# A mixture-of-experts stage whose odd last block of 128 rows joins the last full tile

## Chip, cores and metric

The kernel runs on 1 core of one Trainium2 chip. The metric is device microseconds of one execution, median of several runs.

## What is computed

An adaLN block: layer norm, modulation by rows of `mod`, a gated linear recurrence with projections (the first part, not touched here), a second layer norm, and a mixture of 8 experts with 2 chosen per token. The touched part is the experts:

```
gate_scores = softmax(x @ Wg + bg)
topk_scores, topk_idx = top_k(gate_scores, 2)       # normalized to sum 1
for e in range(8):
    h = gelu(x @ W1[e] + b1[e])                     # 256 -> 1024
    y = h @ W2[e] + b2[e]                           # 1024 -> 256
    output = output + y * combine_w[..., e:e + 1]
x = x + gb * output
```

x has 4 x 1024 tokens of 256 values, float32. The gate's bias is large in these inputs, so the experts get very different numbers of tokens.

## The kernel before

The first part sorts tokens by expert: each token's row goes twice, by an indirect DMA, into a DRAM table `disp_x`, at its place in its expert's region. The second part walks over the experts n = 0 to 7 and over the tiles of each. A tile is TE = 256 rows, two blocks of 128. How many tiles an expert has is known only on the chip: `counts` on DVE packs the numbers, and every engine reads them into registers (`counts_of`, `count_of`) and runs the same loop, `tile(True, 2)`, a hardware loop over `tile(False, 2)`, and, if the number of blocks is odd, `tile(False, 1)` (lines 258 to 267). Each engine has its own copy of `tile`, and they meet at semaphores; `due(name, by)` raises a register and waits for the semaphore to reach it.

In one tile:

- **SP** (388 to 395) loads the rows of the tile into `xin`, one tile ahead, and with an expert's first tile the weights of the expert after next.
- **PE** (932 to 944): layer 1 for f = 0 to 7, six matmuls each (two halves k of the contraction, times three products of high and low parts, because each operand is split into two fp32r numbers), into `mm[f % 4]`, always TE = 256 columns, for an odd block too. Layer 2 follows four f behind, three matmuls per block of 128 rows and f, into `yb`. Behind layer 2 of f = 4 stands `turn()`: four transposes of the next tile's rows into `tp`. Then layer 2 of f = 5, 6, 7.
- **ACT** (743 to 755): two gelus per f, `h32` (double buffered) and its rounded form `hh`; in an expert's first tile a high part of the next expert's weights with f = 4 to 7; at the end `fh`, the high part of the turned rows.
- **DVE** (1256 to 1305): per f the low part `hl`, a small operation on the weights of the tokens, and in an expert's first tile splits of the next expert's weights (`SH` 229, `SL` 237). At the end `fl`, the low part of the turned rows (1239); then a wait for `gbr`, the copy of the rows' last columns (`xm`, 1244), `ytmp` (1295, layer 2 plus bias) and per block `ysb` (1304).
- **POOL** (561 to 578): in an expert's first tile three splits of the next expert's weights (237); then per block an indirect DMA that adds `ysb` to the rows of `out_x` (543), and between the two the gathers of `gbr` for the next tile (538).

What orders the work around the change: POOL's queue holds splits, adds and gathers in program order, two adds never run at once (`y_sent0`, `y_sent1`), and PE's second layer needs `hl` from DVE and an empty `yb` (`y_taken`).

## Time and profile before

| | |
|---|---|
| median of 3 runs | 799.66 us (799.52 to 799.69) |
| profiled execution | 806.43 us |
| its span | 804.6 us |
| TensorE clock granted, mean | 0.942 |
| PE matmul busy | 716.1 us, 89% |
| DVE busy | 559.6 us, 70% |
| ACT busy | 419.0 us, 52% |
| POOL busy | 403.9 us, 50% |

The expert stage begins at about 336.7 us of the span and lasts to its end. Matmuls are pipelined, and the busy time of one is longer than the distance to the next, so a busy TensorE does not tell how fast it goes; distances between starts do. The granted clock is 1.00 at 2.4 GHz and 0.50 at 1.2 GHz.

### The profile page before, as it was taken

What the parts mean: (1) busy time and instruction counts of PE and PEld (TensorE: products, weight loads), DVE (VectorE), ACT (ScalarE), POOL (GpSimd) and SP (SyncE); (2) the same over time, 40 slices, a digit from 0 to 9 for tenths busy, and PEclk for the clock granted to TensorE, in tenths of its full rate; (3) what the DMA queues carried; (4) which work ended last, traced back from release to release, by engine and by line L of the source; (5) the groups of instructions that cost most, each with busy time, mean ns of one, the idle gap of its engine ahead of it and who ended that gap; (6) DMA issues with size and microseconds to landing.
All of it is one profiled execution on the core that took longest, in us unless ns stands there. A gap on an engine that the chain in (4) does not pass through costs nothing.

```text
span 804.6 us, 17323 instructions
## 1 busy us (share of the span) xinstructions
PE 716.1 (89%) x4850; PEld 659.4 (82%) x4850; DVE 559.6 (70%) x1786; ACT 419.0 (52%) x1080; POOL 403.9 (50%) x312
## 2 busy tenths in 40 slices
PE   4999999889799992479999999999898998999992
PEld 1777888778688872369999899998898998999992
DVE  6789888998888659565555755576875576585551
ACT  6365565445455261155665565664554574565660
POOL 1364637666562744734544534554653553553543
PEclk9899999999999995599999999999898999999997
DMA  8531103020101206414455334564532553533432
GB/s 289 185 106 53 54 33 114 28 81 28 53 28 55 81 21 218 166 48 68 71 118 127 60 58 75 117 170 117 154 59 54 118 127 67 106 61 68 65 69 41
DMA packets 50165, 72.56 MB, mean 90 GB/s; under 512 B 5792, under 2 KB 41964, under 8 KB 49968
## 3 DMA queue, kind: packets, MB, share of 16 engines
q0 software_dynamic: 16480, 27.28, 18.5%
q1 hardware_dynamic: 33616, 44.46, 17.5%
q8 instruction: 30, 0.49, 0.3%
q14 instruction: 39, 0.32, 0.1%
HBM read 48.85 MB, written 22.87 MB: 89 GB/s over the span
## 4 chain that ended last, share of the span: by engine, by line
PE 63%; DVE 20%; issue 8%; DMA 3%; ACT 2%; POOL 2%; DVEq 0%; SPq 0%; POOLq 0%; ACTq 0%
PE mm L917 21%; PE yb L927 19%; PE mm L773 14%; PE yb L798 4%; DVE hl L1273 2%; PE tp L900 2%; DMA gbr<-mod_rows,xm 2%; DVE SL L237 1%; DVE nt L954 1%; DVE nt L950 1%; DVE bst L959 1%; PE tp L823 1%; DVE rsn L955 1%; DVE ob L1022 1%; DVE SH L229 1%
## 5 line engine op out<-in xcount | busy, mean ns | idle before, releaser
L750 ACT ACTIVATE h<-mm,b1T 128x256 f32<-128x256 f32 (+1 forms) x288 | 134.2, 466 | 190.8 <-PE mm L917 130.5
L1273 DVE TENSOR_TENSOR hl<-h,hh 128x256 fp32r<-128x256 f32 (+1 forms) x288 | 126.0, 442 | 141.7 <-ACT hh L751 111.5
L543 POOL DMA_INDIRECT out_x<-ysb,tokb x68 | 113.3, 1666 | 204.0 <-DVE ysb L1304 166.4
L917 PE MATMUL mm<-fh,SH 128*128 128x256 f32 x576 | 167.9, 291 | 16.4 <-DVE fl L1239 13.8
L927 PE MATMUL yb<-SH,hh 128*128 128x256 f32 x544 | 158.1, 291 | 10.4 <-DVE hl L1273 10.0
L917 PE MATMUL mm<-fl,SH 128*128 128x256 f32 x576 | 166.0, 288 | 0.0
L917 PE MATMUL mm<-fh,SL 128*128 128x256 f32 x576 | 165.7, 288 | 0.0
L927 PE MATMUL yb<-SH,hl 128*128 128x256 f32 x544 | 154.2, 284 | 0.6 <-issue 0.6
L927 PE MATMUL yb<-SL,hh 128*128 128x256 f32 x544 | 153.5, 282 | 0.0
L751 ACT ACTIVATE hh<-mm,b1T 128x256 fp32r<-128x256 f32 (+1 forms) x288 | 133.5, 464 | 0.0
L917 PEld LDWEIGHTS mm<-fh,SH 128*128 128x128 f32 x576 | 114.2, 198 | 19.1 <-issue 18.4
L773 PE MATMUL mm<-xh,WH 128*128 128x512 f32 x256 | 109.0, 426 | 6.4 <-DVE ob L1022 4.2
L917 PEld LDWEIGHTS mm<-fl,SH 128*128 128x128 f32 x576 | 113.8, 198 | 0.0
L927 PEld LDWEIGHTS yb<-SH,hh 128*128 128x128 f32 x544 | 103.2, 190 | 12.8 <-DVE hl L1273 12.0
L917 PEld LDWEIGHTS mm<-fh,SL 128*128 128x128 f32 x576 | 113.6, 197 | 0.0
L927 PEld LDWEIGHTS yb<-SH,hl 128*128 128x128 f32 x544 | 103.5, 190 | 0.7 <-issue 0.7
L927 PEld LDWEIGHTS yb<-SL,hh 128*128 128x128 f32 x544 | 103.6, 190 | 0.0
L773 PE MATMUL mm<-xh,WL 128*128 128x512 f32 x256 | 103.2, 403 | 0.0
L773 PE MATMUL mm<-xl,WH 128*128 128x512 f32 x256 | 102.7, 401 | 0.0
L538 POOL DMA_INDIRECT gbr<-mod_rows,xm x74 | 76.9, 1039 | 22.6 <-issue 22.6
L498 POOL DMA_INDIRECT disp_x<-h2all,pos x64 | 62.7, 980 | 30.6 <-issue 27.5
L773 PEld LDWEIGHTS mm<-xh,WH 128*128 128x128 f32 x256 | 49.8, 195 | 17.7 <-issue 5.8
(213 smaller groups left out, 1214.9 us busy)
## 6 DMA issues: line engine op xcount, KB each, us to landing
xin<-disp_x SPq DMA_DIRECT2D x74, 132.0 KB
wraw<-in_L_ffn_W SPq DMA_DIRECT2D x8, 1024.0 KB
h2all<-in_L_ffn_W SPq DMA_DIRECT2D x8, 1024.0 KB
xb<-in_L_attn_x SPq DMA_DIRECT2D x8, 512.0 KB, 6.7
out_x<-x2b SPq DMA_DIRECT2D x8, 512.0 KB
mb<-mod_rows SPq DMA_DIRECT2D x3, 768.0 KB, 6.4
wraw<-in_L_attn_W_ugg SPq DMA_DIRECT2D x1, 1536.0 KB, 10.0
gbr<-mod_rows,xm POOLq DMA_INDIRECT x74
```

Source lines behind the costliest of these rows:

```text
L229: e.tensor_copy(SH[n % 2][:, r], wraw[n % 2][:, r]).then_inc(done, 1)
L498: e.indirect_dma_start(out=Xd, out_offset=bass.IndirectOffsetOnAxis(ap=p[:, j:j + 1], axis=0), in_=h2all[:, j, :], in_offset=None).then_in ...
L538: e.indirect_dma_start(out=gbr[:, j, :], out_offset=None, in_=modd.rearrange("b (n d) -> (b n) d", d=D), in_offset=bass.IndirectOffsetOnAx ...
L543: e.indirect_dma_start(out=out_rows, out_offset=bass.IndirectOffsetOnAxis(ap=tokb[:, j:j + 1], axis=0), in_=ysb[:, j, :], in_offset=None, ...
L750: e.activation(h32[:, f % 2, c_], mm[f % 4][:, c_], ACT.Gelu_apprx_tanh, bias=bias)
L751: e.activation(hh[:, f, c_], mm[f % 4][:, c_], ACT.Gelu_apprx_tanh, bias=bias)\
L773: i = e.matmul(mm[q][:, :], a[:, k, c0:c0 + 128], b[:, g % 2, k, :], start=(k == 0 and t == 0), stop=(k == 1 and t == 2))
L798: i = e.matmul(yb[j // 2][:, (j % 2) * D:(j % 2 + 1) * D], og[:, n % 2, j * 128:(j + 1) * 128], wog[:, (g // 2) % 2, hc, :], start=(hc == ...
L900: i = e.transpose(tp[k][:, j * 128:(j + 1) * 128], xin[:, j, k * 128:(k + 1) * 128], ident[:, :])
L917: i = e.matmul(mm[f % 4][:, 0:TE], a[:, k, f * 128:(f + 1) * 128], b[:, k, :], start=(k == 0 and t == 0), stop=(k == 1 and t == 2))
L927: i = e.matmul(yb[0][:, j * D:(j + 1) * D], a[:, f, j * 128:(j + 1) * 128], b[:, f, :], start=(f == 0 and j == 0 and t == 0), stop=(f == N ...
L1273: e.tensor_tensor(hl[:, f, w_], h32[:, f % 2, w_], hh[:, f, w_].bitcast(F32), ALU.subtract)\
```

## The change

A tile with three blocks takes the place of a full tile and an odd one. `count_of` takes one full tile away from the loop when the count of blocks is odd, and behind the loop stands `tile(False, 3)`. Buffers get a third block (`xin`, `xm`, `gbr`, `ysb`, `ytmp` and so on) or 384 columns (`fh`, `fl`, `h32`, `hh`, `hl`, T3 = 384). The third block's rows are loaded with the two others, but turned and split into high and low when the joined tile begins, since the turn at the end of a tile is the same code for all. Layer 1 of f = 0 is cut in 256 and 128 columns, so that it can begin before the third block is there; f = 1 to 7 run over 384 columns. The third block's second layer goes to `yb[1]`. POOL gathers the third `gbr` at the tile's start and makes three adds, then waits for the third to land.

```
@@ -253,6 +256,8 @@
             e.reg_alu(k, half, 1, ALU.logical_shift_right)
             e.reg_alu(k, k, 15, ALU.bitwise_and)
             e.reg_alu(half, half, 1, ALU.bitwise_and)
+            e.reg_alu(k, k, half, ALU.subtract)
+            e.reg_alu(k, k, 1, ALU.max)
             return e.snap(k, min_val=1, max_val=CAP // TE - 1), half
 
         def more_tiles(e, rs, n, tile):
@@ -260,7 +265,7 @@
             with e.Fori(0, k):
                 tile(False, 2)
             with e.If_ne(half, 0):
-                tile(False, 1)
+                tile(False, 3)
 
         def tiles(e, rs, n, tile):
...
@@ -387,6 +392,8 @@
 
                 def tile(first, parts):
                     load(rows_of)
+                    if parts == 3:
+                        e.dma_start(xin[:, 2, :], rows_of(2)).then_inc(S["third_loaded"], 16)
                     if first and n == 0:
                         e.wait_ge(S["counts_ready"], 2)
                         e.reg_load(r_last, nmint[0:1, n:n + 1])
...
+            def gather_gb(j, name):
+                e.indirect_dma_start(out=gbr[:, j, :], out_offset=None, in_=modd.rearrange("b (n d) -> (b n) d", d=D),
+                                     in_offset=bass.IndirectOffsetOnAxis(ap=xm[:, j, 5:6].bitcast(I32), axis=0))\
+                    .then_inc(S[name], 16)
 
             def gather():
...
@@ -562,20 +572,24 @@
                     if first and n + 1 < E:
                         for q in range(5, 8):
                             split_low(e, n + 1, q)
+                    if parts == 3:
+                        due("third_copied", 1)
+                        gather_gb(2, "third_gb")
                     due("y_ready", 1)
                     if not (first and n == 0):
                         due("y_sent0", 0)
                         due("y_sent1", 0)
                     add(0)
-                    if parts == 2:
+                    due("y_ready", 1)
+                    gather()
+                    due("y_sent0", 16)
+                    add(1)
+                    e.reg_add(rl["y_sent1"], rl["y_sent1"], 16)
+                    if parts == 3:
                         due("y_ready", 1)
-                    gather()
-                    if parts == 2:
-                        due("y_sent0", 16)
-                        add(1)
-                        e.reg_add(rl["y_sent1"], rl["y_sent1"], 16)
-                    else:
-                        e.reg_add(rl["y_sent0"], rl["y_sent0"], 16)
+                        due("y_sent1", 0)
+                        add(2)
+                        due("y_sent2", 16)
 
                 tiles(e, ks, n, tile)
             due("gb_loaded", 32)
...
+            def third_part():
+                for k in range(2):
+                    due("third_turned", 1)
+                    e.activation(fh[:, k, TE:T3], tp[k][:, TE:T3], ACT.Copy).then_inc(S["third_high"], 1)
 
             e.reg_mov(rl["rows_turned"], 2)
             e.sem_inc(S["gelu_done"], 4)
@@ -742,6 +761,8 @@
             for n in range(E):
                 def tile(first, parts):
                     c_ = slice(0, 128 * parts)
+                    if parts == 3:
+                        third_part()
                     for f in range(NF):
                         due("layer1_done", 1)
...
@@ -910,12 +931,22 @@
                 w2h, w2l = (t[s][:, 2048:4096].rearrange("p (c n) -> p c n", c=NF) for t in (SH, SL))
                 split_done(e, n)
 
+                def turn_third():
+                    due("third_loaded", 16)
+                    for k in range(2):
+                        e.transpose(tp[k][:, TE:T3], xin[:, 2, k * 128:(k + 1) * 128], ident[:, :])\
+                            .then_inc(S["third_turned"], 1)
+
                 def layer1(f, parts):
                     due("gelu_done", 1)
-                    for k in range(2):
-                        for t, (a, b) in enumerate(((w1h, fh), (w1h, fl), (w1l, fh))):
-                            i = e.matmul(mm[f % 4][:, 0:TE], a[:, k, f * 128:(f + 1) * 128], b[:, k, :],
-                                         start=(k == 0 and t == 0), stop=(k == 1 and t == 2))
+                    cuts = (0, 128 * parts) if parts == 2 or f else (0, TE, T3)
+                    for c0, c1 in zip(cuts, cuts[1:]):
+                        if c0:
+                            due("third_low", 2)
+                        for k in range(2):
+                            for t, (a, b) in enumerate(((w1h, fh), (w1h, fl), (w1l, fh))):
+                                i = e.matmul(mm[f % 4][:, c0:c1], a[:, k, f * 128:(f + 1) * 128], b[:, k, c0:c1],
+                                             start=(k == 0 and t == 0), stop=(k == 1 and t == 2), skip_group_check=True)
                     i.then_inc(S["layer1_done"], 1)
 
                 def layer2(f, parts):
@@ -924,13 +955,15 @@
                     due("hidden_low", 1)
                     for j in range(parts):
                         for t, (a, b) in enumerate(((hh, w2h), (hh, w2l), (hl, w2h))):
-                            i = e.matmul(yb[0][:, j * D:(j + 1) * D], a[:, f, j * 128:(j + 1) * 128], b[:, f, :],
-                                         start=(f == 0 and j == 0 and t == 0), stop=(f == NF - 1 and t == 2),
+                            i = e.matmul(yb[j // 2][:, j % 2 * D:(j % 2 + 1) * D], a[:, f, j * 128:(j + 1) * 128], b[:, f, :],
+                                         start=(f == 0 and j != 1 and t == 0), stop=(f == NF - 1 and t == 2),
                                          skip_group_check=True)
                     i.then_inc(S["layer2_done"], 1)
 
                 def tile(first, parts):
                     due("rows_low", 2)
+                    if parts == 3:
+                        turn_third()
                     for f in range(NF):
                         layer1(f, parts)
                         if f >= 4:
...
+            def third_part():
+                for k in range(2):
+                    due("third_high", 1)
+                    e.tensor_tensor(fl[:, k, TE:T3], tp[k][:, TE:T3], fh[:, k, TE:T3].bitcast(F32), ALU.subtract)\
+                        .then_inc(S["third_low"], 1)
 
+
+            def third_columns():
+                due("third_loaded", 16)
+                e.tensor_copy(xm[:, 2, :], xin[:, 2, D:DW]).then_inc(S["third_copied"], 1)
 
...
+                        5: lambda: e.tensor_scalar(nom[:, 0:2], nom[:, 0:2], float(TE), None, ALU.add),
+                        6: lambda: e.tensor_copy(tokn[:, 0:parts], xm[:, 0:parts, 4].bitcast(I32)),
                     }
                     if first:
-                        mark(e.tensor_scalar(nom[:, :], nom0, float(n * CAP), None, ALU.add))
+                        mark(e.tensor_scalar(nom[:, 0:2], nom0, float(n * CAP), None, ALU.add))
                         due("dve_c", 1)
+                    if parts == 3:
+                        third_columns()
+                        mark(e.tensor_scalar(nom[:, 2:3], nom[:, 1:2], 128.0, None, ALU.add))
+                        third_part()
+                        due("dve_c", 1)
...
@@ -1292,13 +1341,17 @@
                     due("gb_loaded", 32)
                     columns()
                     due("layer2_done", NF)
-                    e.tensor_tensor(ytmp[:, 0:parts, :], yb[0][:, 0:parts * D].rearrange("p (j d) -> p j d", j=parts),
-                                    bc(b2b[:, n, :], parts), ALU.add).then_inc(S["y_taken"], 1)
+                    i = e.tensor_tensor(ytmp[:, 0:2, :], yb[0][:, :].rearrange("p (j d) -> p j d", j=2),
+                                        bc(b2b[:, n, :], 2), ALU.add)
+                    if parts == 3:
+                        i = e.tensor_tensor(ytmp[:, 2, :], yb[1][:, 0:D], b2b[:, n, :], ALU.add)
+                    i.then_inc(S["y_taken"], 1)
                     due("y_taken", 1)
                     for j in range(parts):
-                        sent = "y_sent1" if j else "y_sent0"
-                        if not (first and n == 0):
-                            due(sent, 16)
+                        if j < 2 and not (first and n == 0):
+                            due(f"y_sent{j}", 16)
+                        if j == 2:
+                            due("third_gb", 16)
                         mark(e.tensor_copy(tokb[:, j:j + 1], tokn[:, j:j + 1]))
                         due("dve_c", 1)
                         e.scalar_tensor_tensor(ysb[:, j, :], ytmp[:, j, :], wB[:, j:j + 1], gbr[:, j, :],

```

The new order at the places concerned follows, first POOL, around the end of an expert whose count is odd and the start of the next one. Before, the odd tile's add and gathers and then the splits:

```order
L262 COMPARE_AND_BRANCH
...
L543 DMA out_x<-ysb,tokb 4096x256 [waits s_y_ready,s_y_sent0,s_y_sent1]
...
L538 DMA gbr<-mod_rows,xm 128x256 [waits s_meta_copied]
L538 DMA gbr<-mod_rows,xm 128x256
...
L262 UNCONDITIONAL_BRANCH
L237 TENSOR_TENSOR SL<-wraw,SH 128x512 [waits s_split_high2] x3
```

After, the joined tile and then the same splits (line numbers are those of the changed file; L553 is the add, L543 the gather):

```order
L543 DMA gbr<-mod_rows,xm 128x256 [waits s_third_copied]
...
L553 DMA out_x<-ysb,tokb 4096x256 [waits s_y_ready,s_y_sent0,s_y_sent1]
...
L281 REGISTER_ALU [waits s_y_ready]
L543 DMA gbr<-mod_rows,xm 128x256 [waits s_meta_copied]
L543 DMA gbr<-mod_rows,xm 128x256
...
L553 DMA out_x<-ysb,tokb 4096x256 [waits s_y_sent0]
...
L281 REGISTER_ALU [waits s_y_ready]
L553 DMA out_x<-ysb,tokb 4096x256 [waits s_y_sent1]
...
L267 UNCONDITIONAL_BRANCH [waits s_y_sent2]
L240 TENSOR_TENSOR SL<-wraw,SH 128x512 [waits s_split_high2] x3
```

Between the last gather and the splits there are now two more adds and a wait for a landing.

Second, PE at the start of that tile. Before, the odd tile's first layer follows the branch directly:

```order
L262 COMPARE_AND_BRANCH
L276 REGISTER_ALU
L276 REGISTER_ALU [waits s_rows_low]
L917 MATMUL mm<-fh,SH 128x256 [waits s_gelu_done]
L917 MATMUL mm<-fl,SH 128x256
```

After:

```order
L281 REGISTER_ALU [waits s_rows_low]
L937 MATMUL tp<-ident,xin 128x128 [waits s_third_loaded]
L937 MATMUL tp<-ident,xin 128x128
L281 REGISTER_ALU
L948 MATMUL mm<-fh,SH 128x256 [waits s_gelu_done]
...
L948 MATMUL mm<-fh,SH 128x128 [waits s_third_low]
...
L948 MATMUL mm<-fh,SH 128x384 [waits s_gelu_done]
L948 MATMUL mm<-fl,SH 128x384
```

The 128-column matmuls wait for DVE's subtraction, and all of the first layer from f = 1 on stands behind them. On DVE that subtraction stands behind the last tile's output:

```order
L1357 SCALAR_TENSOR_TENSOR ysb<-ytmp,wB,gbr 128x256 [waits s_dve_c]
...
L267 COMPARE_AND_BRANCH
...
L1287 COPY xm<-xin 128x8 [waits s_third_loaded]
L1315 TENSOR_SCALAR nom<-nom 128x1
...
L1278 TENSOR_TENSOR fl<-tp,fh 128x128 [waits s_third_high]
...
L1278 TENSOR_TENSOR fl<-tp,fh 128x128 [waits s_third_high]
```

Before, DVE went from `ysb` straight to `hl` of the next tile.

## Rows read from the trace of the kernel before

**Rows 1.** Groups by line and form: name, count, busy us, mean ns, idle before

```profile
L1295 DVE TENSOR_TENSOR ytmp<-yb,x2b 128x512 f32<-128x512 f32 x32 | 22.1, 691 | 19.2 <-PE yb L927 19.2
L1295 DVE TENSOR_TENSOR ytmp<-yb,x2b 128x256 f32<-128x256 f32 x4 | 1.7, 424 | 0.0
```

**Rows 2.** Windows: length, us busy (count) of PE, PEld, DVE, ACT, POOL; PEclk

```profile
425.23:435.17 9.94, 9.94 (x87) 9.94 (x86) 5.32 (x22) 4.92 (x16) 4.05 (x4) 1.00 0.72 173
435.17:446.69 11.52, 11.21 (x93) 10.81 (x92) 9.54 (x25) 9.31 (x24) 7.34 (x6) 1.00 0.47 83
446.69:462.53 15.84, 13.96 (x102) 13.26 (x101) 10.54 (x28) 6.95 (x19) 7.23 (x6) 0.89 0.28 54
462.53:474.26 11.73, 11.73 (x103) 11.73 (x102) 6.55 (x23) 6.47 (x17) 5.01 (x4) 1.00 0.29 55
```

**Rows 3.** Windows, last row and sum: odd turn to next, then next to second

```profile
700.04:712.36 12.32, 11.18 (x93) 10.78 (x92) 9.40 (x27) 8.95 (x24) 7.30 (x6) 1.00 0.47 80
sum 46.90, PE 44.78 PEld 43.17 DVE 36.97 ACT 36.34 POOL 27.74; mean PE 11.20 PEld 10.79 DVE 9.24 ACT 9.08 POOL 6.93
...
712.36:727.66 15.30, 13.81 (x102) 13.41 (x101) 9.95 (x26) 7.48 (x20) 7.33 (x6) 0.89 0.30 53
sum 62.38, PE 54.98 PEld 53.29 DVE 42.62 ACT 28.57 POOL 31.24; mean PE 13.74 PEld 13.32 DVE 10.66 ACT 7.14 POOL 7.81
```

**Rows 4.** Timeline, PE: start us, length us; nine and 29 matmuls between the pairs

```profile
99.72 0.39 PE L773 MATMUL mm<-xl,WH 128*128 128x512 f32 x1
...
101.78 0.39 PE L773 MATMUL mm<-xl,WH 128*128 128x512 f32 x1
...
427.79 0.28 PE L917 MATMUL mm<-fh,SH 128*128 128x256 f32 x1
...
431.18 0.27 PE L917 MATMUL mm<-fh,SL 128*128 128x256 f32 x1
```

**Rows 5.** Timeline, PE: two stops, idle before in brackets

```profile
449.73 0.38 PE L927 MATMUL yb<-SH,hh 128*128 128x256 f32 x1 [1.73 <-DVE hl L1273]
...
605.88 0.58 PE L917 MATMUL mm<-fh,SH 128*128 128x256 f32 x1 [3.81 <-DVE fl L1239]
```

**Rows 6.** Timeline, DVE, around expert 0's odd tile and expert 1's first

```profile
427.99 0.69 DVE L1295 TENSOR_TENSOR ytmp<-yb,x2b 128x512 f32<-128x512 f32 x1 [1.09 <-PE yb L927]
...
429.00 0.48 DVE L1304 SCALAR_TENSOR_TENSOR ysb<-ytmp,wB,gbr 128x256 f32<-128x256 f32 x1
...
430.04 0.49 DVE L1273 TENSOR_TENSOR hl<-h,hh 128x128 fp32r<-128x128 f32 x2
...
437.85 0.18 DVE L1244 COPY xm<-xin 128x16 f32<-128x16 f32 x1 [0.56 <-DMA gbr<-mod_rows,xm]
...
438.70 0.48 DVE L1304 SCALAR_TENSOR_TENSOR ysb<-ytmp,wB,gbr 128x256 f32<-128x256 f32 x1
...
444.38 4.37 DVE L1264 TENSOR_SCALAR nom<-nom 128x2 f32<-128x2 f32 x1
```

**Rows 7.** Timeline, POOL, the same stretch

```profile
430.64 1.56 POOL L543 DMA_INDIRECT out_x<-ysb,tokb  x1 [4.92 <-DVE ysb L1304]
...
433.82 0.99 POOL L538 DMA_INDIRECT gbr<-mod_rows,xm  x1 [0.30 <-issue]
...
435.50 1.61 POOL L543 DMA_INDIRECT out_x<-ysb,tokb  x1 [0.69 <-issue]
...
440.33 1.71 POOL L543 DMA_INDIRECT out_x<-ysb,tokb  x1 [3.22 <-DMA out_x<-ysb,tokb]
...
444.94 3.77 POOL L237 TENSOR_TENSOR SL<-wraw,SH 128x512 fp32r<-128x512 f32 x3
```

**Rows 8.** POOL's adds into out_x, from issue to landing

```profile
DMA to landing us min/median/max: 3.7/3.9/4.7
```

**Rows 9.** Windows behind two stops, columns as in the second group

```profile
451.55:454.60 3.05, 2.94 (x14) 2.65 (x14) 2.34 (x8) 0.68 (x2) 0.00 (x0) 0.50 0.33 83
...
605.88:611.38 5.50, 5.50 (x26) 5.50 (x27) 2.89 (x9) 2.52 (x6) 2.58 (x2) 0.50 0.36 69
```

More of the change, by code:

```diff
@@ L20 @@
 TE = 256
+T3 = 384
 MW = 8
@@ L537, in gather @@
                 for j in range(2):
-                    e.indirect_dma_start(out=gbr[:, j, :], out_offset=None, in_=modd.rearrange("b (n d) -> (b n) d", d=D),
-                                         in_offset=bass.IndirectOffsetOnAxis(ap=xm[:, j, 5:6].bitcast(I32), axis=0))\
-                        .then_inc(S["gb_loaded"], 16)
+                    gather_gb(j, "gb_loaded")
             def add(j):
```

62 lines of the change are left out of this document (31 added, 31 removed).

## Prediction

> **What bounds the kernel.** I read the page first: TensorE is busy for most of the span, but that figure hides where it waits, so the expert stage has to be cut by tiles. The DVE line that adds the second layer's bias runs once a tile and has one form per kind of tile: 32 full tiles and 4 of one block [rows 1]. Its start times give the experts: experts 0, 1, 4 and 5 end in an odd block, the other four do not. So the change acts at four places.
>
> Next the windows between turns (the transposes of the next tile's rows, once a tile on PE) [rows 2]. T is a turn's time. From turn to turn a full tile has 96 matmuls and takes 11.73 us (11.72 in most others), 9.94 us when the 81 matmuls between the turns before and in an odd tile are meant. The pitch from one matmul start to the next is (431.18 - 427.79) / 29 = 0.117 us at 256 columns and (101.78 - 99.72) / 9 = 0.229 us at 512 [rows 4]. So 96 x 0.1175 = 11.28 us, and 0.44 us is left for a turn: PE is the bound in a steady tile, with no slack of its own.
>
> What breaks this are two stretches after an odd block [rows 2, 3]. From the odd tile's turn to the next, 87 matmuls should take 10.66 us; the four stretches sum to 46.90, 4.26 us too much. The odd tile's second layer leaves 9 matmuls (1.1 us) behind the turn, less than the copy and subtraction of the turned rows take. From the first tile's turn of the next expert to the second's, the four sum to 62.38, 15.5 us over four steady tiles: PE stops for hl [rows 5], because DVE's instruction stood for 4.37 us [rows 6] while POOL ran its three splits in 3.77 us [rows 7]. After such a stop the granted clock is 0.50, that is 1.2 GHz in place of 2.4, for a while [rows 9].
>
> **The change, part by part.**
>
> (a) Matmuls. An odd tile goes: 48 + 24 matmuls of 256 columns and a turn, 72 x 0.1175 + 0.44 = 8.90 us. Its 24 second-layer matmuls come back in the joined tile (2.82 us). Of the first layer 42 matmuls grow to 384 columns; midway between 0.117 and 0.229 is 0.173, so 42 x 0.056 = 2.35 us. Six of 128 columns are new; no row shows that form, so the bounds are half of 0.117 and 0.117, and I take 0.09 (0.54 us). Two transposes, 0.2 us. Together 5.9 us, so 3.0 us are saved per odd block, 12.0 in all. This is real PE time and nothing hides it.
>
> (b) The short tail. The joined tile has 27 matmuls behind its turn instead of 9 (3.2 us), more than the fh and fl chain needs. The 4.26 us go: -4.3.
>
> (c) The third block's rows, a new wait. They are turned only when the joined tile begins, and DVE subtracts them only behind the last tile's output. In a full tile ytmp starts at T + 2.76, ysb at T + 3.77, and DVE's next instruction at T + 4.81 [rows 5, 6]. There the small copy and two subtractions of 128 columns come in (0.1 each for the small ones, about 0.25 each for the others), so fl is there at T + 5.6. PE has begun the tile at T + 2.56, and two transposes and six matmuls last it to T + 3.5. So it waits some 2.0 us. ACT and the DMA of the rows are no part of this: that load is issued a tile ahead. Behind the waiting PE instruction stand L1(1) to L1(4), which were what covered DVE's lateness before. Behind the stop of about 2 us at 449.73 came 14 matmuls at the half clock (3.05 / 14 = 0.218 us each) [rows 9], behind others of nearly that length none: 14 x 0.096 = 1.35 us, counted half, 0.65. Four times 2.65: +10.6.
>
> (d) POOL. An odd tile's POOL work ended with its gathers; nobody waited for its add. The joined tile ends in three adds, each waiting for the landing of the one before, and a wait for the last landing, and behind that stand the three splits of the next expert, the next tile's add and its gathers. From the joined tile's turn T' on: 27 matmuls, ytmp at T' + 3.9; the extra block puts the first ysb at T' + 5.3; add 0 comes 1.6 us after its ysb (438.70 to 440.33 in that tile, and 429.00 to 430.64 here [rows 6, 7]): T' + 6.9. Add 1 follows 4.8 later (430.64 to 435.50 [rows 7], with two gathers inside): T' + 11.7. Landing takes 3.9 us [rows 8] and about 0.6 more until POOL's next: add 2 at T' + 16.2, last landing seen at T' + 20.7. Splits 3.9: T' + 24.6. The next tile's add 0 at 24.8, second gather 3.2 after it (430.64 to 433.82) at 28.0; it lands 4.0 later (DVE stood for the one of 433.82 until 437.85 [rows 6, 7]): T' + 32.0. DVE, in the second tile of the next expert, wants it at about T' + 26 and has nothing to do instead. Then ytmp, ysb 0 (33.2), the landing of add 1 (24.8 + 4.8 + 4.3 = 33.9), ysb 1, and hl for the third tile is ready at T' + 35.0. PE undisturbed would want it at T' + 3.7 + 2 x 11.72 + 5 x 6 x 0.1175 = T' + 30.7. That is 4.3 us of standing still, and like the 3.81 us stop of 605.88 it should be followed by 26 matmuls at 0.50, 5.50 / 26 = 0.21 us each in place of 0.1175 [rows 5, 9]: 26 x 0.096 = 2.5. So 6.8 us a time, 27.2 for four. Against that the old stalls of the first tiles go, 15.5, since the splits no longer fall there. In expert 5 the late tile is itself a joined one and PE meets the wait five matmul groups sooner, about 1 us more. Together +12.7.
>
> Costed at nothing: wider gelus (ACT 0.36 to about 0.47 us each, two per 2.1 us of PE), wider hl, and SP's third load per joined tile, which SP issues with a tile's time in hand. If that cover went, 6 x 0.2 us would show.
>
> Sum: -12.0 - 4.3 + 10.6 + 12.7 = **+7.0 us**. Against the profiled execution (806.43 us, a span of 804.6 and 1.8 around it) that is 813.4; that execution is 6.8 above the median of the runs, and I carry the difference over: 799.66 + 7.0 = 806.7.
>
> **The rivals.**
>
> R1, the price of POOL's chain is about that of the old stalls. Each link in (d) has a spread of about half a microsecond and there are four; if all are short, the stop is 2 to 2.5 us and the clock seldom falls. Then (d) is near zero and the rest gives -5.7: 794. For it: landings reach down to 3.7 [rows 8]. Against: nothing in the chain overlaps.
>
> R2, the other side in full: the chain is absorbed. The place is DVE's wait for the gathers in the second tile of the next expert, the price 6.8 us each, and it decides at T' + 30.7: if the chain is over 4.3 us shorter, old stalls of 15.5 us disappear and only a lateness of 1 us in the first tile is left. Then -12.0 - 4.3 + 10.6 - 15.5 + 4 = -17: 782. For it: DVE has half its time free. Against: the rows of landings. The Trainium skill, "DMA: Bandwidth & Descriptors", section "Anatomy of one DMA", puts the fixed part of a transfer, setup and completion, at some 2.0 us. By that, four landings of 2 us would take 7.6 us off the chain and R2 would hold. The row of this trace has 3.7 at the least and 3.9 in the middle, so this rule of the Trainium skill does not fit these adds, and the measurement decides.
>
> R3, worse than forecast: dependent adds come at over 5 us, or expert 2, which has only two tiles, carries the lateness into the first tile of expert 3, where DVE also splits weights. 2 to 3 us more per place: 816 and up.
>
> R4, the change is not taken (no odd block reaches the new branch): 799.7. The four forms of 256 columns speak against it [rows 1].
>
> **How the numbers follow.** Forecast 0.58, with a range of its own of 800.5 to 816; R1 0.18; R2 0.12; R3 0.10; R4 0.02. A measurement of this kernel can tell about 0.2%, 1.6 us, from no change. Faster takes R1 and R2: 0.30. Same takes R4 and the low edge of the forecast: 0.06. Slower: 0.64. The range reaches down to R1 and up to the edge of R3: 793 to 816; R2 and most of R3 stay outside.
>
> **What would show it.** (a) 36 turns become 32; matmuls of 384 columns with a pitch near 0.173. (b) no stop between joined tile and next expert but some tenths. (c) four stops of about 2 us in front of the 128-column matmuls, ended by DVE fl. (d) POOL's splits some 20 us behind the joined tile's turn, DVE's copy xm idle for 4 to 6 us on gbr in the second tile, PE idle about 4 us for hl or yb in the third. The forecast is wrong if the third tile after a joined one runs at 11.7 us, or if the stop in (c) is under 1 us.

## The result, and the profile after

| | before | after |
|---|---|---|
| median of 4 runs each | 799.67 us (799.52 to 801.37) | 815.06 us (813.57 to 817.61) |
| ratio | | 1.0193 (95% interval 1.0174 to 1.0211) |
| profiled execution | 806.43 us | 816.36 us |
| its span | 804.6 us | 814.6 us |
| TensorE clock granted, mean | 0.942 | 0.932 |
| TensorE matmul busy | 716.1 us, 89% | 711.4 us, 87% |

The change makes the kernel slower by 15.4 us in the medians and by 10.0 us between the two profiled executions. Forecast were +7.0 and a range of 793 to 816. So the sign held, the range held by 0.9 us, and the size was less than half of what came. For the profiled execution the forecast was 813.4 us, and it took 816.36. A second comparison, below, gave 1.0158. Two of all the runs below were in the chip's slower state (802.10 us in `e6_dve_cut4`, 1185.47 us in `e10_before_dve_again`), and the times and ratios leave them out.

In the changed program layer 1 is line 948, layer 2 line 958, `fl` 1272 and the third block's `fl` 1278, `hl` 1322, the copy `xm` 1283, `ysb` 1357, the splits 240, the adds 553 and the gathers 543.

The page of the changed kernel: its busy shares, and the chain of work that ended last.

```profile
span 814.6 us, 16564 instructions
...
PE 711.4 (87%) x4674; PEld 655.7 (80%) x4674; DVE 547.1 (67%) x1734; ACT 410.0 (50%) x1016; POOL 398.2 (49%) x308
...
PE 56%; DVE 15%; DMA 10%; issue 9%; POOL 6%; ACT 2%; POOLq 1%; SPq 0%; DVEq 0%; ACTq 0%
PE yb L958 17%; PE mm L948 16%; PE mm L794 14%; DMA out_x<-ysb,tokb 7%; PE yb L819 4%; POOL gbr L543 1%; POOL SL L240 1%; PE tp L921 1%; DVE rsn L988 1%; POOL disp_x L505 1%; DVE hl L1322 1%; DVE ob L1055 1%; DVE bst L992 1%; PE tp L844 1%;
```

TensorE is busy for 4.7 us less and the end comes 10 us later. The landing of an add into `out_x` is now 7% of the chain, some 57 us: the adds have become part of what sets the end. In the chain of before all DMA together had 3%.

The windows between turns: first the four joined tiles, from the turn ahead of each to its own T', then the turn to turn stretches behind the first of them (these answer to [rows 2, 3]). Columns: stretch, its length, busy time of PE, its weight loads, DVE, ACT and POOL, granted clock, DMA share, GB/s.

```profile
411.90:430.86 18.96, 17.18 (x126) 16.98 (x124) 8.40 (x27) 9.54 (x20) 7.41 (x6) 1.00 0.50 112
509.38:529.87 20.49, 18.71 (x125) 18.51 (x124) 8.41 (x27) 9.54 (x20) 8.15 (x6) 0.92 0.47 104
631.56:652.06 20.50, 18.72 (x126) 18.52 (x124) 8.40 (x27) 9.54 (x20) 6.74 (x6) 0.92 0.44 104
677.17:706.55 29.38, 20.16 (x126) 19.95 (x125) 8.82 (x27) 9.54 (x20) 14.54 (x12) 0.77 0.30 50
...
430.86:444.16 13.30, 13.15 (x111) 12.94 (x110) 9.95 (x33) 7.96 (x20) 5.31 (x4) 1.00 0.26 49
444.16:455.97 11.81, 11.81 (x103) 11.81 (x102) 9.87 (x23) 7.15 (x19) 6.05 (x5) 1.00 0.29 49
```

The third stretches, in which POOL's chain arrives:

```profile
455.97:473.96 17.99, 14.55 (x103) 14.35 (x102) 7.09 (x25) 7.78 (x20) 10.21 (x8) 0.81 0.46 73
555.04:573.88 18.84, 13.61 (x102) 13.12 (x101) 9.86 (x32) 8.03 (x20) 9.46 (x8) 0.91 0.66 177
731.65:750.54 18.89, 14.49 (x102) 14.29 (x101) 6.75 (x23) 7.48 (x20) 9.90 (x8) 0.82 0.44 71
```

Expert 5 has three tiles, so its third stretch is itself a joined tile, the one of 29.38 us. The first stretch (13.30) has nothing of the old idle in it, and the second runs at the steady pace, where before it cost 3.6 to 4.1 us more [rows 2]. The time comes back one tile later: 6.3 to 7.2 us above a steady tile of before.

TensorE's queue in the joined tile of expert 0, and in the third stretch behind it:

```profile
417.32 0.33 PE L948 MATMUL mm<-fh,SH 128*128 128x128 f32 x1 [1.78 <-DVE fl L1278]
417.48 0.28 PE L948 MATMUL mm<-fl,SH 128*128 128x128 f32 x1
...
417.94 0.27 PE L948 MATMUL mm<-fh,SL 128*128 128x128 f32 x1
...
418.27 0.34 PE L948 MATMUL mm<-fl,SH 128*128 128x384 f32 x1
...
419.86 0.34 PE L948 MATMUL mm<-fl,SH 128*128 128x384 f32 x1
...
465.69 0.58 PE L958 MATMUL yb<-SH,hh 128*128 128x256 f32 x1 [3.44 <-DVE hl L1322]
466.07 0.41 PE L958 MATMUL yb<-SL,hh 128*128 128x256 f32 x1
...
471.19 0.32 PE L958 MATMUL yb<-SL,hh 128*128 128x256 f32 x1
```

The stop in front of the 128-column matmuls is there. The pitch, the distance from one matmul's start to the next, is (419.86 - 418.27) / 9 = 0.177 us for 384 columns and (417.94 - 417.48) / 4 = 0.115 us for 128. Behind the 3.44 us stop the matmuls go at (471.19 - 466.07) / 24 = 0.213 us, the half clock, as in [rows 9].

What POOL does from T' = 430.86 on, in the order in which it comes:

```profile
437.67 1.58 POOL L553 DMA_INDIRECT out_x<-ysb,tokb  x1 [11.17 <-DVE ysb L1357]
...
442.35 1.62 POOL L553 DMA_INDIRECT out_x<-ysb,tokb  x1 [0.38 <-issue]
447.40 1.56 POOL L553 DMA_INDIRECT out_x<-ysb,tokb  x1 [3.43 <-DMA out_x<-ysb,tokb]
451.32 4.29 POOL L240 TENSOR_TENSOR SL<-wraw,SH 128x512 fp32r<-128x512 f32 x3 [2.36 <-DMA out_x<-ysb,tokb]
455.76 1.55 POOL L553 DMA_INDIRECT out_x<-ysb,tokb  x1 [0.16 <-issue]
...
458.93 0.99 POOL L543 DMA_INDIRECT gbr<-mod_rows,xm  x1 [0.30 <-issue]
```

and what DVE waits for meanwhile:

```profile
462.20 0.17 DVE L1283 COPY xm<-xin 128x16 f32<-128x16 f32 x1 [4.24 <-DMA gbr<-mod_rows,xm]
```

| link, us behind T' | forecast | here |
|---|---|---|
| add 0 | 6.9 | 6.8 |
| add 1 | 11.7 | 11.5 |
| add 2 | 16.2 | 16.5 |
| splits | 20.7 | 20.5 |
| next tile's first add | 24.8 | 24.9 |
| its second gather | 28.0 | 28.1 |
| copy `xm` | 32.0 | 31.3 |
| TensorE goes on | 35.0 | 34.8 |

Every link is within 0.7 us of the forecast here. The chain that starts in expert 4's joined tile and ends in expert 5's was slower. Its last add goes out together with SP's load of 1024 KB of weights, and POOL's splits then wait for that add to land:

```profile
669.69 1.57 POOL L553 DMA_INDIRECT out_x<-ysb,tokb  x1 [3.11 <-DMA out_x<-ysb,tokb]
669.71 0.43 SPq L300 DMA_DIRECT2D h2all<-in_L_ffn_W  x1
676.12 3.98 POOL L240 TENSOR_TENSOR SL<-wraw,SH 128x512 fp32r<-128x512 f32 x3 [4.85 <-DMA out_x<-ysb,tokb]
```

```profile
690.06 0.48 PE L948 MATMUL mm<-fh,SH 128*128 128x128 f32 x1 [9.22 <-DVE fl L1278]
```

There T' is 652.06. Adds 1 and 2 came at T' + 12.7 and 17.6 (11.7 and 16.2 forecast) and the splits at T' + 24.1 in place of 20.7: the add of 669.69 took 6.2 us to land, the longest of the 36 adds whose landing was traced, where the median is 3.8. The windows of the third add at the first place and at this one, columns as above, differ in what the DMA engines moved:

```profile
447.40:451.32 3.92, 3.92 (x35) 3.92 (x34) 2.56 (x9) 2.76 (x8) 1.56 (x1) 1.00 0.54 105
669.69:676.12 6.43, 6.43 (x57) 6.43 (x56) 3.81 (x14) 4.87 (x14) 1.57 (x2) 1.00 0.81 229
```

It was the same place in two more traces: in `c_after` the add of 673.03 took 5.4 us beside a load of 672.51, in `e1_wait_later` the add of 670.38 took 6.6 us beside a load of 670.83. So this is most likely the weight load in the way, and not the scatter of one execution; no run moved the load, so that is not shown.

### The profile page after: what moved, and what is told of

It is laid out like the page before. It is cut to its first block, busy times and chain, and to the rows that moved or that the text cites. A ratio compares the mean times of both kernels' runs of the same rounds, so it can differ in the third digit from the quotient of the medians.

```text
span 814.6 us, 16564 instructions
## 1 busy us (share of the span) xinstructions
PE 711.4 (87%) x4674; PEld 655.7 (80%) x4674; DVE 547.1 (67%) x1734; ACT 410.0 (50%) x1016; POOL 398.2 (49%) x308
## 3 DMA queue, kind: packets, MB, share of 16 engines
q1 hardware_dynamic: 33040, 43.92, 16.8%
## 4 chain that ended last, share of the span: by engine, by line
PE 56%; DVE 15%; DMA 10%; issue 9%; POOL 6%; ACT 2%; POOLq 1%; SPq 0%; DVEq 0%; ACTq 0%
PE yb L958 17%; PE mm L948 16%; PE mm L794 14%; DMA out_x<-ysb,tokb 7%; PE yb L819 4%; POOL gbr L543 1%; POOL SL L240 1%; PE tp L921 1%; DVE rsn L988 1%; POOL disp_x L505 1%; DVE hl L1322 1%; DVE ob L1055 1%; DVE bst L992 1%; PE tp L844 1%; POOL out_x L553 1%
## 5 line engine op out<-in xcount | busy, mean ns | idle before, releaser
L771 ACT ACTIVATE h<-mm,b1T 128x256 f32<-128x256 f32 (+1 forms) x256 | 125.4, 490 | 187.6 <-PE mm L948 138.8
L553 POOL DMA_INDIRECT out_x<-ysb,tokb x68 | 110.8, 1629 | 217.3 <-DVE ysb L1357 175.2
L1322 DVE TENSOR_TENSOR hl<-h,hh 128x256 fp32r<-128x256 f32 (+1 forms) x256 | 120.6, 476 | 115.9 <-ACT hh L772 113.7
L958 PE MATMUL yb<-SH,hh 128*128 128x256 f32 x544 | 159.3, 293 | 16.5 <-DVE hl L1322 16.5
L948 PE MATMUL mm<-fh,SH 128*128 128x256 f32 (+2 forms) x520 | 156.6, 301 | 19.5 <-DVE fl L1278 14.6
L948 PE MATMUL mm<-fh,SL 128*128 128x256 f32 (+2 forms) x520 | 154.7, 297 | 3.6 <-issue 3.6
L948 PE MATMUL mm<-fl,SH 128*128 128x256 f32 (+2 forms) x520 | 155.7, 299 | 0.0
L772 ACT ACTIVATE hh<-mm,b1T 128x256 fp32r<-128x256 f32 (+1 forms) x256 | 124.8, 488 | 0.0
L948 PEld LDWEIGHTS mm<-fh,SH 128*128 128x128 f32 x520 | 103.7, 200 | 24.7 <-DVE fl L1278 15.4
L948 PEld LDWEIGHTS mm<-fl,SH 128*128 128x128 f32 x520 | 103.5, 199 | 0.0
L948 PEld LDWEIGHTS mm<-fh,SL 128*128 128x128 f32 x520 | 103.5, 199 | 0.0
L543 POOL DMA_INDIRECT gbr<-mod_rows,xm x70 | 71.8, 1026 | 21.3 <-issue 21.3
## 6 DMA issues: line engine op xcount, KB each, us to landing
wraw<-in_L_attn_W_ugg SPq DMA_DIRECT2D x1, 1536.0 KB, 11.7
```

The lines of the kernel that those rows point to most:

```text
L543: e.indirect_dma_start(out=gbr[:, j, :], out_offset=None, in_=modd.rearrange("b (n d) -> (b n) d", d=D), in_offset=bass.IndirectOffsetOnAx ...
L553: e.indirect_dma_start(out=out_rows, out_offset=bass.IndirectOffsetOnAxis(ap=tokb[:, j:j + 1], axis=0), in_=ysb[:, j, :], in_offset=None, ...
L771: e.activation(h32[:, f % 2, c_], mm[f % 4][:, c_], ACT.Gelu_apprx_tanh, bias=bias)
L772: e.activation(hh[:, f, c_], mm[f % 4][:, c_], ACT.Gelu_apprx_tanh, bias=bias)\
L948: i = e.matmul(mm[f % 4][:, c0:c1], a[:, k, f * 128:(f + 1) * 128], b[:, k, c0:c1], start=(k == 0 and t == 0), stop=(k == 1 and t == 2), s ...
L958: i = e.matmul(yb[j // 2][:, j % 2 * D:(j % 2 + 1) * D], a[:, f, j * 128:(j + 1) * 128], b[:, f, :], start=(f == 0 and j != 1 and t == 0), ...
```

## The experiments

Each time stands beside runs of the kernel before on the same chip. That kernel took 798.7 to 807.0 us from one comparison to the next, so ratios are compared and not times. A ratio here is the recorded estimate with its 95% interval, which is not the plain quotient of the two medians. `c_before`, `e1_wait_later`, `e3_buffers` and `e4_before_dve` ran beside a kernel before of 805.79 us; `c_after`, `e2_cut4`, `e5_after_dve` and `e8_buffers_pad`, on the same chip, beside 807.00; `e6_dve_cut4`, `e10_before_dve_again` and a single run of `e11_hh_only`, on another chip, beside 804.64; and a single run of `e12_fh_only`, on a third one, beside 798.67.

**The two kernels again.** No edit.

> The kernel before once more, as a second profile of it. Both theories: ratio 1.000 within 0.002, a steady tile of 11.72 us from turn to turn, and again 15 to 16 us of excess over the four first tiles behind odd blocks. If the first profile of it was an unusual one (it was 6.8 us above the median), the stretch ahead of the experts or behind the last turn is 3 us shorter here, or a first tile ran without a clock drop.

> The changed kernel once more, beside the three others of this job and the kernel before on one chip. Both theories: ratio 1.012 to 1.020, turns of the tiles behind a joined one 13.3, 11.8 and 18 to 19 us apart, an extra 10 us in expert 5's joined tile.

The kernel before against itself: 805.47 us, ratio 1.000 (0.9978 to 1.0022). The changed kernel: 819.5 against 807.0 us, ratio 1.0158 (1.0106 to 1.0211). So these comparisons can tell about 0.2% to 0.6%, depending on how many runs they have, and the loss is there again: 12.5 us in the medians. In the trace of `c_after` the first three joined tiles took 18.95, 18.97 and 18.97 us: the same stop in front of the 128-column matmuls each time (1.76 to 1.78 us idle), and no half clock behind it. In the trace of the changed kernel two of three had one (20.49, 20.50).

**Does the chain of waits set the late stop?** The changed kernel; POOL waits for the third block's landing behind the next expert's splits, not ahead of them.

```
@@ POOL, tile @@
+                    if first and n:
+                        due("y_sent2", 0)
...
                         add(2)
-                        due("y_sent2", 16)
+                        e.reg_add(rl["y_sent2"], rl["y_sent2"], 16)
...
+            due("y_sent2", 0)
```

> The changed kernel, with POOL's wait for the landing of the third add moved behind the three splits of the next expert. Theory (POOL's chain sets the stop in the third tile): splits start some 4 us sooner, at about T' + 16.7, the gather of the second tile lands 4 us sooner, and the stop of 3.4 us and more in the third tile goes. But the splits then fall on the ysb and the first hl of the second tile, DVE stands for 4 us there, and PE stops some 3 us in the second tile instead, with a half clock behind it in most: about 803 us, ratio 1.005. Rival (the third tile's lateness comes from DVE's own longer list behind a joined tile): the stop stays where it is, 815 us.

814.08 us, ratio 1.0101 (1.0066 to 1.0135). Windows behind the first joined tile, columns as above, and the three instructions that matter:

```profile
418.26:437.22 18.96, 17.18 (x126) 16.98 (x124) 8.51 (x27) 9.52 (x20) 8.23 (x6) 1.00 0.52 113
437.22:450.53 13.31, 13.16 (x112) 12.95 (x110) 9.96 (x33) 7.78 (x20) 5.37 (x4) 1.00 0.26 50
450.53:467.92 17.39, 13.66 (x102) 13.31 (x101) 11.94 (x25) 8.26 (x21) 10.68 (x8) 0.90 0.35 56
```

```profile
454.30 4.80 DVE L1360 SCALAR_TENSOR_TENSOR ysb<-ytmp,wB,gbr 128x256 f32<-128x256 f32 x1
```

```profile
454.51 4.29 POOL L240 TENSOR_TENSOR SL<-wraw,SH 128x512 fp32r<-128x512 f32 x3
```

```profile
460.75 0.58 PE L961 MATMUL yb<-SH,hh 128*128 128x256 f32 x1 [3.73 <-DVE hl L1325]
```

The stop left the third stretch and came a tile earlier, into the second. The splits now run while DVE makes `ysb`, and DVE's instruction takes 4.80 us in place of 0.48. So the place of the splits decides where TensorE stands, and an earlier place only trades the wait for a landing against the shut-out of [rows 6, 7]. In expert 5 the joined tile took 20.50 us in place of 29.38. I had expected a ratio of about 1.005; each second stretch cost 5.1 to 5.6 us over a steady one (17.39, 17.24, 16.86 and 17.06 us), more than I had counted for it.

**Without POOL's splits.** In both kernels the low parts q = 5, 6, 7 of the next expert's weights move from POOL to DVE, behind `columns()` and ahead of `ytmp` in the first tile.

```
@@ POOL, tile @@
-                    if first and n + 1 < E:
-                        for q in range(5, 8):
-                            split_low(e, n + 1, q)
@@ DVE, tile @@
+                    if first and n + 1 < E:
+                        for q in range(5, 8):
+                            split_low(e, n + 1, q)
```

> The changed kernel with the three low parts moved from POOL to DVE, as in the run that gave 0.971 for the kernel before. Theory (POOL's chain of adds, landings and splits makes the stop in the third tile): without the splits the chain is 4.1 us shorter, hl is ready at T' + 31 against a need at T' + 31, so the third tile has a stop of less than 1 us and no half clock, and no first tile has the old stops. From 0.971 come off 12 us of matmuls and 4 of short tail, and on it come 7 of stops in the joined tiles, 4 of clock and 2.5 of buffers: about 0.968. Rival (the joining itself costs time somewhere else, in the joined tile or on the queues): 0.98 or more, still 9 us or so above what the kernel before has with the same move.

> The kernel before, with the three low parts of the next expert's weights (q = 5, 6, 7) computed by DVE, behind its copy xm in an expert's first tile, in place of POOL. Theory (the old stops come from DVE being shut out while POOL splits): the stops of 1.7 to 3.8 us and the half clocks behind them go in all first tiles, some 25 us in all, less a small lateness of ytmp, since 1.9 us of DVE work meet 1.1 us of idle time there: 774 to 780 us, ratio 0.97 to 0.975. Rival (the first tile is simply too much for DVE): the 1.9 us come on top and the stops stay, near 800 or above.

> The kernel before with DVE's low parts, run again beside the last one on the same chip. Both theories: ratio 0.967 to 0.976. If the run with both remedies is below it by more than the intervals, joining pays; if the two are within 0.3%, it pays nothing here.

Changed kernel so edited: 794.34 us, ratio to the kernel before 0.9848 (0.9795 to 0.99). Kernel before so edited: 784.22 us, 0.9713 (0.9666 to 0.9761), and again on another chip 787.60 us, 0.9751 (0.9691 to 0.981). This is the best version of the study, faster than both kernels; I had expected 0.97 to 0.975. Windows of both, from the full tile ahead of expert 0's last block. The kernel before so edited (odd tile, then two stretches of expert 1):

```profile
437.21:448.62 11.41, 11.21 (x94) 10.81 (x93) 8.93 (x30) 9.02 (x24) 5.49 (x4) 1.00 0.53 81
448.62:460.46 11.84, 11.84 (x102) 11.78 (x101) 8.78 (x26) 6.52 (x17) 4.48 (x4) 1.00 0.33 60
460.46:472.21 11.75, 11.75 (x103) 11.75 (x102) 6.45 (x22) 6.96 (x18) 6.13 (x5) 1.00 0.43 71
```

The changed kernel so edited (joined tile, then three stretches; last the joined tile of expert 5):

```profile
417.79:438.33 20.54, 18.73 (x125) 18.53 (x124) 8.39 (x27) 9.53 (x20) 7.03 (x6) 0.92 0.48 103
438.33:451.65 13.32, 13.17 (x111) 12.96 (x110) 9.96 (x33) 7.79 (x20) 5.39 (x4) 1.00 0.29 50
451.65:464.55 12.90, 12.30 (x103) 11.94 (x102) 9.29 (x28) 8.17 (x21) 5.55 (x4) 1.00 0.38 58
464.55:476.36 11.81, 11.81 (x103) 11.81 (x102) 6.42 (x22) 6.21 (x16) 7.08 (x5) 1.00 0.46 83
668.18:689.85 21.67, 18.72 (x125) 18.51 (x124) 8.61 (x27) 9.64 (x20) 8.16 (x7) 0.92 0.36 61
```

In the kernel before the old stall is gone: 11.84 us where [rows 2] have 15.84. The three other places have 12.46, 11.73 and 11.90; in `e10_before_dve_again` one of the four is back at 15.82, with a stop of 2.30 us for `hl`. In the changed kernel the third stretch is 11.81 in place of 17.99, the two others 13.98 and 13.14, and the joined tile of expert 5 takes 21.67 in place of 29.38. So the late stop needs both the chain of adds and the splits behind it. But with the splits gone from both, the joined version is still 10 us behind. I had expected 0.968; what came is the rival's ratio, of 0.98 or more. From the turns of the two traces: at the four places the joined tile and the stretch behind it cost 135.1 us, against 132.9 for a full tile, an odd one and the stretch behind; the second stretches cost 3.7 us more and the third ones 3.1. In the first tile of an expert DVE now makes the three splits ahead of `ytmp`; the kernel before has room for that behind an odd block (11.84), the joined version, whose DVE comes out of three outputs, has not (12.90). That is read from the order of the work; no run tested it.

**Without the third block's wait.** The changed kernel; f = 0 to 3 of a joined tile all run over 256 columns first, then over the 128 of the third block.

```
+                def layer1_cut():
+                    for c0, c1 in ((0, TE), (TE, T3)):
+                        if c0:
+                            due("third_low", 2)
+                        for f in range(4):
...
```

> The changed kernel with the first layer of f = 0 to 3 cut, all four over 256 columns first and then all four over the third block's 128, so that 24 matmuls (2.8 us) and not 6 lie ahead of the wait for the third block's rows. Theory (the 1.8 us stop in a joined tile is DVE's lateness, and the half clock follows from the stop): the four stops go, three of them with 1.3 us of half clock, and 18 further matmuls of 128 columns replace the growth to 384, (0.112 - 0.060) x 18 = 0.9 us per joined tile. About 7 us less in all, ratio 1.004 to 1.012. Rival (the third block's chain through ACT and DVE is what is slow, some 3 us behind the start of the tile): the stop shrinks but stays. The third tile behind a joined one keeps its stop under both.

814.82 us, ratio 1.0129 (1.0068 to 1.019) against the 1.0158 of `c_after` on the same chip. I had expected 1.004 to 1.012. The median is 4.7 us below that of `c_after`, but the intervals overlap, so the times do not settle it and the trace has to.

```profile
417.13:435.03 17.90, 17.90 (x143) 17.90 (x142) 8.40 (x27) 9.08 (x20) 7.30 (x6) 1.00 0.55 119
448.35:460.69 12.34, 12.06 (x102) 11.86 (x101) 10.60 (x25) 7.89 (x21) 6.18 (x5) 1.00 0.29 49
460.69:475.96 15.27, 12.08 (x102) 11.88 (x101) 6.72 (x24) 6.69 (x18) 9.82 (x8) 1.00 0.48 75
```

TensorE is busy through the whole joined tile (17.90 of 17.90), and its 24 matmuls of 128 columns come at (423.93 - 422.81) / 10 = 0.112 us:

```profile
422.81 0.28 PE L958 MATMUL mm<-fl,SH 128*128 128x128 f32 x1
...
423.93 0.28 PE L958 MATMUL mm<-fh,SL 128*128 128x128 f32 x1
```

The wait for the third block's rows, (c) of the prediction, is real and can be covered, but the 18 further matmuls take half of it back: three cuts of six, each pair of 256 and 128 columns (0.1183 + 0.112) in place of one of 384 (0.176), 18 x 0.054 = 0.98 us. That leaves 1.05 us a tile (18.95 in `c_after`), 4.2 in all.

**Both remedies.** The changed kernel with the splits on DVE and the four cuts.

> The changed kernel with both remedies: DVE computes the three low parts, and the first layer of f = 0 to 3 is cut. Theory (what joining costs is the chain of POOL and the stop for the third block; the matmuls it saves are real): the joined tile's turn comes 17.9 us behind the last one, not 19 to 20.6, with no half clock, so about 10 us less than with DVE's low parts alone (0.985): 0.970 to 0.975, no better than the kernel before with DVE's low parts (0.971), because DVE has three outputs in a row ahead of the next expert's first tile and is late by about 1 us in that expert's second tile. Rival (joining pays once both are mended): 0.965 or less.

788.67 us (three runs, 786.50 to 791.41), ratio 0.9786 (0.9748 to 0.9823). On the same chip the kernel before with the splits moved had 0.9751. The intervals overlap, so with all its waits treated the joined tile is not shown to be faster than the tile of its own, and I had expected a little more from it (0.970 to 0.975). In the trace the joined tiles are now cheap (19.58, 17.92, 17.90, 18.50 us), but TensorE stood twice with nothing it waited for, at its first matmul of expert 3 (1.96 us) and of expert 4, the second time with 25 matmuls at half clock behind it:

```profile
587.86 0.58 PE L942 MATMUL mm<-fh,SH 128*128 128x256 f32 x1 [3.31 <-issue]
```

**Larger buffers alone.** A steady tile takes 11.80 to 11.81 us in the changed kernel and 11.72 before. The kernel before with the third block's buffers and nothing else of the change; then the same with 32 bytes ahead of `fh`; then 384 columns for `hh` and `hl` alone, and for `fh` and `fl` alone.

```
-            fh = sb(p2, "fh", [128, 2, TE], F32R)
+            fh = sb(p2, "fh", [128, 2, T3], F32R)
...
-            hh = sb(p2, "hh", [128, NF, TE], F32R)
+            hh = sb(p2, "hh", [128, NF, T3], F32R)
...
+            pad = sb(p2, "pad", [128, 8])
```

> The kernel before with nothing but the larger buffers of the change (third block, 384 columns), each used at its old size; the computation and the order of the work are those of before. If the sizes or addresses of the buffers make the steady tile longer (11.81 in place of 11.72 us in the two profiles), it is 11.81 here too and the time is 2 to 3 us above before, ratio 1.003. If not, 11.72 and ratio 1.000.

> The kernel before with the larger buffers and 32 bytes of padding ahead of fh, so that fh, fl, hh and hl start at 32 past a multiple of 64 bytes again, as in the kernel before; in the changed kernel they start at a multiple of 64, like the weights SH and SL. Theory A (where these buffers start relative to the weights decides): steady tile 11.72 us and an odd tile 9.95. Theory B (the distance between their rows, 384 columns, decides): still 11.80 and 10.03. The whole time differs by 2.6 us between the two, less than the runs scatter, so the turns decide it.

> The kernel before with hh and hl alone at 384 columns a row (used at 256). Theory B1 (the distance between rows of the second layer's stationary operand costs the 0.08 us): steady tile 11.80 us. Theory B2 (it is fh and fl, the first layer's moving operand, or where any of the buffers lie): 11.72.

> The kernel before with fh and fl alone at 384 columns a row (used at 256). If the row distance of the first layer's moving operand costs the 0.08 us a tile, the steady tile is 11.80 us here; hh and hl alone gave 11.72. If 11.72, it is neither operand by its row distance but where the buffers lie.

Larger buffers: 805.63 us, ratio 0.9996 (0.9973 to 1.002), a steady tile of 11.81. With the pad: 807.76 us, 1.0003 (0.9975 to 1.003), 11.80 to 11.86, so no return to 11.72. `hh` and `hl` alone: one run of 804.11, 11.72. `fh` and `fl` alone: one run of 799.26, against 798.67 on that chip, 11.72. So the slower pitch comes with the buffers, not with the code, and it was in each of the kernels that had all of them. A shift of `fh` by 32 bytes does not take it away, and the row distance of one pair alone does not make it. Whether sizes or places make it, and of which buffer, stays open. Its price is 0.08 us a tile; in the times of `e3_buffers` it does not show, and in its trace the four first tiles behind odd blocks took 56.0 us, where `c_before` had 61.7.

## Why the prediction was right in sign and short in size

The ledger of the expert stage, from the second turn to the last one of each profiled execution (366.57 to 786.33 before, 364.67 to 797.77 after): 419.76 and 433.10 us, so +13.3 where my sum was +7.0. Of the 8.4 us that the medians lie above the forecast, 6.3 are in this stage; 3.4 went the other way outside it, and 5.5 are the carry-over from profiled execution to median. The step of the sum that failed most is (a) + (b), the matmuls saved and the short tail: put at -16.3, it measured -12.8.

| term | forecast | measured |
|---|---|---|
| (a) + (b) matmuls and short tail | -16.3 | -12.8 |
| (c) first three joined tiles | +8.0 | +9.3 |
| (d) third stretches | +20.4 | +20.5 |
| (c) + (d) expert 5's joined tile | +10.5 | +12.5 |
| (d) old stalls gone | -15.5 | -15.5 |
| steady and second tiles, 19 x 0.08 | 0 | +1.5 |
| expert 4's second tile | 0 | -2.2 |
| sum | +7.0 | +13.3 |

Where the time comes from: before, the four places took 86.7 us for full and odd tile and 46.90 [rows 3] for the stretch behind, 133.6 in all. A joined tile without its stop takes 16.9 by the pitches: 69 x 0.1183 + 6 x 0.115 + 42 x 0.1765, and 0.64 for transposes. `e2_cut4`, where nothing stops, gives the same: 17.90 - 0.98. The four stretches behind the joined tiles took 53.3. So 4 x 16.9 + 53.3 = 120.9, hence 12.8 us less by unrounded numbers. The pair of `c_before` and `c_after` gives -12.9 for this term and +12.1 for the stage.

(a) and (b), the step that was mis-sized most. A joined tile should have been 16.55 us and was 16.9: 42 matmuls of 384 columns at 0.1765 and not 0.173 (0.15 us), six of 128 at 0.115 and not 0.09, nearly the upper bound (0.15), and the wider steady pitch (0.06). So (a) gave 10.6 us and not 12.0. And I let "the 4.26 us go" with nothing in their place: with 105 matmuls the stretch behind should have been 12.8 us and was 13.3. In it TensorE came to the first `hl` too early and lost 0.4 us (0.31 ahead of that matmul and 0.10 behind it), because DVE had three outputs to make first. So (b) gave 2.2 us and not 4.3.

(c) was right. A stop with 1.78 us idle in the profile costs some 2.06 (18.96 - 16.9), since the pitch is shorter than a matmul's modelled length and the first starts behind a pause are wider. I had 2.0. The half clock behind it came in two of three joined tiles here, in none of three in `c_after`, in two of three in `e5_after_dve` and in one of three in `e1_wait_later`, at 1.5 us each. With 5 of 12 half weight was near the mean, and this execution had more.

(d) was right link by link at the first place, in `c_after` the three third stretches come to 19.7 us, and `e1_wait_later` and `e5_after_dve` show that it was the cause: moving the splits moves the stop, and taking them away removes it. Only expert 5 was under-sized: 10.5 us, where 12.5 came. There the chain was 3.4 us longer, 2 of them by the landing of 6.2 us beside the weight load. I had taken the median landing for all links and had not looked at what else is under way when an add lands.

Not in the sum at all: the slower pitch of steady tiles, +1.5 (wider buffers were no step of mine at all), and expert 4's second tile, which lost part of its old stall, 16.31 us for 18.44. In expert 3's first tile there was another loss that the ledger hides inside the third stretch: a stop of 3.60 us in the middle of six matmuls, with nothing waited for.

```profile
561.97 0.28 PE L948 MATMUL mm<-fh,SL 128*128 128x256 f32 x1 [3.60 <-issue]
```

It stood ahead of the chain's wait in that stretch, which was then short (1.63 us, where the other two third stretches have 3.44 and 4.40), so most of it seems to have cost nothing: the stretch took 18.84 us, the two others 17.99 and 18.89.

From the stage to the execution: behind the last turn the changed kernel had 16.8 us left, and 18.3 before, a gain of 1.5 that I did not foresee and cannot explain (POOL's last add starts 10.0 us behind the last turn in both, so it lies behind that); the six traces with a joined tile have 16.8 to 17.3 there, the eight others 18.3 to 18.4; and the second turn came 1.9 us earlier. That one is scatter of the first part, which the change does not touch: over the fourteen traces of the study it came anywhere from 362.3 to 371.0, with and without the change. So 13.3 - 1.5 - 1.9 = +9.9, the +10.0 of the spans. The rest of the way to 15.4 is the carry-over, the largest single part of the miss and no part of the mechanism: the profiled execution before was 6.8 us above the median of its runs, and I assumed that the changed kernel's would be too. It was 1.3 above. Single runs of the kernel before on one chip came between 802.5 and 810.3 us, so the distance of one execution from a median could not be carried over. That the range still held is in part luck: the 3.4 us outside the stage had no term and took back more than half of what the stage cost beyond the sum.

The rivals: R1 and R2 needed a short chain and fell; the chain took 34.8 us of the forecast 35.0. The rule of the Trainium skill ("DMA: Bandwidth & Descriptors", section "Anatomy of one DMA") by which R2 would have held did not fit: the adds landed in 3.7 to 6.2 us, median 3.8, not some 2. R3 came true in part, at one place: dependent adds of more than 5 us apart in expert 4's joined tile, at 2.0 us. The lateness that it expects in expert 3 did not come: the tile from 573.88 took 17.75 us, and 17.64 before. R4 fell at once, since forms of 384 columns are there.

## What to carry to other kernels

Count what stands behind the last of a chain of dependent DMAs on its queue, not only the chain: here nobody waited for the odd block's add, until it became the third of a chain with three splits and two gathers behind its landing. And look at what large loads fall on such a chain: the long landings of three traces lie beside one. A tile saved on the busiest engine saves its matmuls, but also removes the slack in which slower engines caught up; price that slack as the wait that follows. And the cheap cure was in the old stall: moving three splits from POOL to DVE, which had stood still while they ran, gave 2.5% to 2.9% in the kernel before, and no form of the joined tile that was tried added anything to that.

## What was not expected of the hardware

- **Short matmuls hardly get shorter.** Starts of 128, 256, 384 and 512 columns of this type (fp32r, with a weight load for each) are 0.112, 0.118, 0.176 and 0.229 us apart, the last by [rows 4]: from 256 up the pitch follows the columns, below it does not. The 0.112 is that of `e2_cut4`. The Trainium skill, "TensorE: Matmul & The Clock Gate", section "Back-to-back issue gap", gives some 0.081 us for 128 columns in a stream of loads and matmuls; the trace does not agree for this type, with 0.112.
- **DVE is shut out for all of POOL's splits at once.** One DVE instruction took 4.80 us (0.48 otherwise) while three POOL instructions ran 4.29 us without a gap. The Trainium skill, "SBUF — State Buffer", section "Who interferes with whom", says that the shared port pair is held for a whole instruction and the other engine blocks; the trace agrees in kind, but DVE did not get in between the three either, though its record begins 0.21 us ahead of theirs.
- **Stops without a wait.** From 370 us on TensorE stood 1.3 to 5.0 us with nothing waited for, 13 times in seven of the eight traces that have a joined tile or DVE's splits (not in `e1_wait_later`), and in none of the six of the kernel before with its splits on POOL. Four stand where the chain's wait would be, and may be that wait. The nine others can't be: they lie between matmuls that wait for nothing, with lengths of 1.3 to 4.6 us. All nine begin within 1 us of where TensorE goes over to a new expert, five at expert 3 (around 562 us) and four at expert 4; experts 2 and 3, just ahead, have two tiles each and skip the code of the odd or joined tile. In each of these nine a transfer of 16 KB on the DMA queue of kind instruction (q8 on the page) starts inside the stop or up to 1.2 us ahead of it, at 559.4 us for the one from 558.4 to 562.0 us in the changed kernel; at the four others there is none. So the loading of code is the suspect. Such transfers also come where nothing stops, and no run took them away, so it is not shown.
- **A pitch that changes with the buffers**, 11.72 or 11.81 us a steady tile, with the same order of work. Whether their sizes or their places do it is open.
